# Prefetched mask tiles, a second set of accumulator banks, and two subtractions on GpSimd in a sandwich layer on eight cores

## The chip, the cores and the metric

The kernel runs on the eight cores of one Trainium2 chip, each with its own 2048 of the 16384 token rows and with all the weights. The metric is the device time of the slowest core in microseconds. Two runs of the kernel before took 3683.49 and 3685.18 us, median 3684.34 us.

## What is computed

```python
def reference(x, w1, mask, w2, bias):
    # mask is cut into blocks of 32x32; a block counts when its sum is > 0
    w_masked = w1 * elem_mask
    x = x + layernorm(einsum('bsk,nk->bsn', layernorm(x), w_masked))
    x = x + layernorm(einsum('bsi,oi->bso', layernorm(x), sign(w2)) + bias)
    return x
```

x is 2 x 8192 x 4096 in float32, w1, w2 and the int32 mask are 4096 x 4096. The products run in bf16.

## The kernel before

Each core takes its tokens in four chunks of 512 (`c`), a chunk in four token tiles of 128 (`tt`), and does the two layers of a chunk one after the other. A layer's weight comes in 16 slabs (`sl`) of 2 MB: `nsl = sl // 2` names one of eight groups of 512 output columns, `kh = sl % 2` a half of the contraction. A slab gives 64 matmuls (four token tiles by 16). The four token tiles of one `nsl` fill the four banks of `pmm`. After the second half DVE copies them to `ARAW` (L458 in layer 0, L461 with the bias in layer 1) and takes statistics (L469). The next `nsl` writes the same four banks, so its first matmul waits for that copy (`ev_at[(nsl - 1, tt)]`). The other four banks, `ptA` and `ptB`, are used for transposes and for small products of the mask.

**Chunk 0** makes the weights as it goes. SP loads float32 pieces of 512 KB into two buffers `WST` (L338). In layer 0, DVE multiplies a piece by the block mask `BTE` into the slab buffer `WSL` (L367), in layer 1 ACT takes the sign (L381). GpSimd stores each finished slab in DRAM as bf16 (L392), and chunks 1 to 3 load it from there (L407), into two slab buffers by turns.

**The mask chain** (`emit_mask_chain`) makes `BTE` for one `nsl`, eight times. For each of four row tiles of the mask GpSimd loads 2 MB (L228, into `OS` seen as int32), adds neighbours in five halving steps from 4096 to 128 columns (L238), ACT converts the 128 columns (L254), and PE and DVE reduce the rows (L267 to L284). The single staging tile and the working tile `MHI` are free for the next row tile once ACT has read `MHI` (`vAs`). At the end the 16 columns pass through DRAM (L297, L306). The chains of `nsl` 0 and 1 stand first in every queue, before the first normalization of x. The chain of `nsl` n+2 is placed behind slab 2n. So on DVE the multiplications of the slabs after it stand behind its four row tiles, and on GpSimd the chain stands behind the store of the slab before.

**Between layers.** `emit_p0` loads a chunk's x by halves of a token tile into two buffers `XS` and normalizes it. Once layer 0 is done, `emit_a2` does for each token tile and half: `ARAW *= r1` (L608), `XP = XS - m` (L610), `XP += ARAW` (L613), all on DVE. Then ACT squares and sums `XP` (L620), DVE works out the scale in some eleven operations of one column (L630 to L645), ACT normalizes into `HS` (L651), PE transposes into `ptA` and `ptB` (L204) and ACT copies to `HT` (L214). `emit_finalize` ends a chunk: for each token tile DVE waits until the output buffer `OS` has been stored (`sO`), then does `ARAW *= r3` (L695), `OS = XP - m` (L697), `OS += ARAW` (L700), and ACT issues the store (L706). The finalization of chunk c stands behind slab 0 of the next chunk on DVE, ahead of the copies out of `pmm`. That of the last chunk ends the program.

Of the kernel before, what the change touches and what calls it, by code (L numbers as in the profile page):

```python
# [19 lines left out]
D = 4096  # L20
# [11 lines left out]
SEMS = ["sW0", "sW1", "sWs0", "sWs1", "sX0", "sX1", "sM", "sC0", "sC1",  # L32
# [5 lines left out]
def build():  # L38
# [16 lines left out]
    with es:  # L55
# [161 lines left out]
        def emit_mask_chain(nsl, first):  # L217
# [3 lines left out]
            def _(g):  # L221
                for r in range(4):
                    rt = nsl * 4 + r
                    if rt == 0:
                        wt(g, bias_os_free)
                    else:
                        g.wait_ge(sem["vAs"], rt)
                    g.dma_start(OSi32[:, :], mask_d[rt * 128:(rt + 1) * 128, :]  # L228
                                ).then_inc(sem["sM"], 16)
                    cnt["sM"] += 16  # L230
                    g.wait_ge(sem["sM"], cnt["sM"])
                    spans = [(0, 2048), (2048, 1024), (0, 512), (2048, 256),
                             (0, 128)]
                    cur = OSi32[:, :]
# [179 lines left out]

        def emit_slab_mm(c, layer, sl, ready, su, ev_at, ht_mark, site,
                         pre_tt=None):
# [4 lines left out]
            def _(t):  # L421
# [4 lines left out]
                for tt in range(NT):  # L426
                    if kh == 0:
                        wt(t, ht_mark(tt))
                        if nsl > 0:
                            wt(t, ev_at.get((nsl - 1, tt)))  # L430
                        elif prev_ev[0] is not None:
                            wt(t, prev_ev[0][tt])
                    for j in range(KTS):
# [3 lines left out]
                        ins = t.matmul(pmm[:, tt * 512:(tt + 1) * 512],  # L437
# [11 lines left out]
            if kh == 1:  # L449
                @blk.vector  # L450
                def _(v):
                    wt(v, ("vFi", state["og"]))
                    ins = None
                    for tt in range(NT):
                        wt(v, mm_marks[tt])
                        dst = ARAW[:, tt * D + nsl * 512: tt * D + (nsl + 1) * 512]
                        if layer == 0:
                            ins = v.tensor_copy(dst,  # L458
                                                pmm[:, tt * 512:(tt + 1) * 512])
                        else:  # L460
                            ins = v.tensor_tensor(dst,  # L461
                                                  pmm[:, tt * 512:(tt + 1) * 512],
# [91 lines left out]
        def emit_a2(c, t0, ev_at):  # L554
            a2_load = {}

            @blk.gpsimd
            def _(g):
                for tt in range(NT):
                    for hf in range(2):  # L560
                        u = state["xs_uses"]
                        state["xs_uses"] += 1
                        g.wait_ge(sem["vXf"], u - 1)
                        sn = "sX%d" % (u % 2)
                        g.dma_start(XS[u % 2][:, :],  # L565
                                    x_d[t0 + tt * 128: t0 + (tt + 1) * 128,
                                        hf * 2048:(hf + 1) * 2048]
                                    ).then_inc(sem[sn], 16)
                        cnt[sn] += 16
# [238 lines left out]
```

## Time and profile before

| | |
|---|---|
| median of two runs | 3684.34 us |
| the profiled execution's own time | 3681.35 us |
| its span on the slowest core (core 3) | 3679.8 us |
| spans of the other cores | 3653.9 to 3668.1 us |
| mean granted TensorE clock, all cores | 0.793 to 0.799 |
| busy in the span | PE 54%, PEld 25%, DVE 24%, ACT 14%, POOL 9% |
| moved by DMA | 573 MB, 156 GB/s in the mean |

All stretches are in microseconds from the start of the span of core 3. PE is TensorE's matmuls and PEld its weight loads, DVE is VectorE, ACT ScalarE, POOL GpSimd, SP the queue of SyncE. A letter q behind an engine's name is its instruction queue. "Idle before" an instruction is followed by what ended the wait.

### The profile page before, as it was taken

What the parts mean: (1) busy time and instruction counts of PE and PEld (TensorE: products, weight loads), DVE (VectorE), ACT (ScalarE), POOL (GpSimd) and SP (SyncE); (2) the same over time, 40 slices, a digit from 0 to 9 for tenths busy, and PEclk for the clock granted to TensorE, in tenths of its full rate; (3) what the DMA queues carried; (4) which work ended last, traced back from release to release, by engine and by line L of the source; (5) the groups of instructions that cost most, each with busy time, mean ns of one, the idle gap of its engine ahead of it and who ended that gap; (6) DMA issues with size and microseconds to landing.
All of it is one profiled execution on the core that took longest, in us unless ns stands there. A gap on an engine that the chain in (4) does not pass through costs nothing.

```text
span 3679.8 us, 24392 instructions; the slowest of 8 cores (3653.9 to 3679.8 us)
## 1 busy us (share of the span) xinstructions
PE 1987.2 (54%) x9296; PEld 931.4 (25%) x9296; DVE 899.8 (24%) x1460; ACT 524.5 (14%) x364; POOL 344.1 (9%) x336
## 2 busy tenths in 40 slices
PE   1011321330334165654499299559919946983992
PEld 0010110110112122222244144224414422432441
DVE  0031220220224200112511411351141134223124
ACT  0030000000000633333100500110050020005000
POOL 2402132233220000000000000000000000000000
PEclk9996655665667587886699599779959977996996
DMA  2235644544555377776434334344333434341442
GB/s 94 101 122 176 184 129 169 172 147 141 184 159 208 92 239 229 242 227 211 182 143 149 125 115 160 137 183 153 144 114 137 160 137 183 144 153 69 160 151 101
DMA packets 72947, 573.16 MB, mean 156 GB/s; under 512 B 8800, under 2 KB 8816, under 8 KB 42112
## 3 DMA queue, kind: packets, MB, share of 16 engines
q1 hardware_dynamic: 50688, 335.57, 27.6%
q0 software_dynamic: 19840, 202.47, 15.2%
q10 hardware_dynamic: 2304, 33.56, 2.3%
q8 instruction: 76, 1.25, 0.1%
q14 instruction: 39, 0.32, 0.0%
HBM read 470.86 MB, written 100.70 MB: 155 GB/s over the span
## 4 chain that ended last, share of the span: by engine, by line
PE 36%; DMA 31%; DVE 11%; ACT 9%; POOL 7%; issue 4%; DVEq 0%; POOLq 0%; ACTq 0%; SPq 0%
PE pmm L437 35%; DMA WST<-w2s 10%; DMA OS<-mask 9%; DMA WST<-w1s 7%; POOL MHI L238 7%; DMA XS<-x 3%; DMA out<-OS 2%; DVE WSL L367 2%; DVE OS L700 2%; ACT WSL L381 2%; ACT HS L651 2%; ACT HS L620 2%; DVE BNST L508 1%; DVE OS L697 1%; PE ptA L204 1%
## 5 line engine op out<-in xcount | busy, mean ns | idle before, releaser
L437 PE MATMUL pmm<-WSL,HT 128*128 128x512 bf16 x8192 | 1846.7, 389 | 362.2 <-ACT WSL L381 195.5
L437 PEld LDWEIGHTS pmm<-WSL,HT 128*128 128x128 bf16 x8192 | 816.0, 100 | 1387.3 <-issue 472.0
L267 PE MATMUL ptB<-COLRED,P4T 128*4 128x128 bf16 x32 | 8.5, 265 | 680.3 <-ACT COLRED L254 680.3
L204 PE MATMUL ptA<-IDN,HS 128*128 128x128 bf16 x576 | 67.2, 310 | 551.0 <-ACT HS L651 304.5
L461 DVE TENSOR_TENSOR ARAW<-pmm,BIASF 128x512 bf16<-128x512 f32 x128 | 88.5, 691 | 991.8 <-PE pmm L437 991.8
L367 DVE TENSOR_TENSOR WSL<-WST,BTE 128x1024 bf16<-128x1024 f32 x128 | 155.7, 1223 | 210.6 <-DMA WST<-w1s 209.3
L458 DVE CAST ARAW<-pmm 128x512 bf16<-128x512 f32 x128 | 85.6, 688 | 487.6 <-PE pmm L437 487.0
L204 PEld LDWEIGHTS ptA<-IDN,HS 128*128 128x128 bf16 x576 | 58.6, 144 | 560.6 <-issue 560.6
L267 PEld LDWEIGHTS ptB<-COLRED,P4T 128*4 128x4 bf16 x32 | 2.6, 80 | 686.1 <-issue 686.1
L381 ACT ACTIVATE WSL<-WST 128x1024 bf16<-128x1024 f32 x128 | 135.1, 1056 | 249.4 <-DMA WST<-w2s 249.2
L280 DVE TENSOR_SCALAR BRT<-ptB 4x128 bf16<-4x128 f32 x32 | 8.9, 279 | 622.4 <-PE ptB L267 622.4
L469 DVE BATCH_NORM_STATS2 BNST<-ARAW 128x6 f32<-128x512 bf16 x256 | 158.3, 680 | 6.6
L620 ACT ACT_TABLE_LOAD x16 | 20.5, 1283 | 924.0 <-DVE XP L613 923.8
L238 POOL TENSOR_TENSOR MHI<-OS 128x2048 int32<-128x2048 int32 x32 | 114.8, 3588 | 309.7 <-DMA OS<-mask 309.7
L238 POOL TENSOR_TENSOR MHI<-MHI 128x1024 int32<-128x1024 int32 (+3 forms) x128 | 125.9, 984 | 18.7 <-POOL MHI L238 0.5
L565 POOL DMA_DIRECT2D XS<-x x32 | 19.5, 609 | 1006.8 <-DVE XP L613 930.4
L508 DVE BATCH_NORM_STATS2 BNST<-XS 128x6 f32<-128x512 f32 x128 | 78.8, 680 | 135.5 <-DMA XS<-x 135.5
L489 POOL DMA_DIRECT2D XS<-x x32 | 16.9, 530 | 735.2 <-ACT HS L540 681.4
L254 ACT ACT_TABLE_LOAD x8 | 10.3, 1283 | 514.2 <-POOL MHI L238 514.2
L214 ACT ACTIVATE HT<-ptA 128x2048 bf16<-128x2048 bf16 x36 | 67.6, 1877 | 79.5 <-PE ptA L204 79.5
L540 ACT ACT_TABLE_LOAD x4 | 5.1, 1283 | 511.4 <-DVE AUX L522 511.4
L700 DVE TENSOR_TENSOR OS<-OS,ARAW 128x4096 f32<-128x4096 f32 x16 | 70.8, 4425 | 1.7
(54 smaller groups left out, 742.6 us busy)
## 6 DMA issues: line engine op xcount, KB each, us to landing
WSL<-c1m SPq DMA_DIRECT2D x48, 2048.0 KB, 8.9
WSL<-c2m SPq DMA_DIRECT2D x48, 2048.0 KB, 8.8
WST<-w1s SPq DMA_DIRECT2D x128, 512.0 KB, 4.8
OS<-mask POOLq DMA_DIRECT2D x32, 2048.0 KB, 8.9
XS<-x POOLq DMA_DIRECT2D x64, 1024.0 KB, 6.0
WST<-w2s SPq DMA_DIRECT2D x128, 512.0 KB, 4.9
c1m<-WSL POOLq DMA_DIRECT2D x16, 2048.0 KB, 10.1
c2m<-WSL POOLq DMA_DIRECT2D x16, 2048.0 KB, 10.6
```

The lines of the kernel that those rows point to most:

```text
L204: ins = t.transpose(pt[:, j * 128:(j + 1) * 128], HS[:, ktg * 128:(ktg + 1) * 128], IDN[:, :])
L238: ins = g.tensor_tensor(MHI[:, dst_off:dst_off + dst_n], a[:, :, 0], a[:, :, 1], op=OP.add)
L367: ins = v.tensor_tensor(dst, src, mk, op=OP.mult)
L381: ins = s.activation(buf[:, j0 * 512:(j0 + KTQ) * 512], WST[(wfirst + q) % 2][:, :], AF.Sign)
L437: ins = t.matmul(pmm[:, tt * 512:(tt + 1) * 512], st_ap, mv_ap, start=(kh == 0 and j == 0), stop=(kh == 1 and j == KTS - 1))
L458: ins = v.tensor_copy(dst, pmm[:, tt * 512:(tt + 1) * 512])
L461: ins = v.tensor_tensor(dst, pmm[:, tt * 512:(tt + 1) * 512], BIASF[:, nsl * 512:(nsl + 1) * 512], op=OP.add)
L469: ins = v.bn_stats(BNST[:, sslot * 48 + nsl * 6: sslot * 48 + (nsl + 1) * 6], ARAW[:, tt * D + nsl * 512: tt * D + (nsl + 1) * 512])
L508: ins = v.bn_stats(bn[:, (hf * 4 + q) * 6: (hf * 4 + q + 1) * 6], xb[:, q * 512:(q + 1) * 512])
L620: ins = s.activation(HS[:, :], XP[:, tt * D:(tt + 1) * D], AF.Square, accum_out=XSQ[:, tt:tt + 1])
L651: ins = s.activation(HS[:, :], XP[:, tt * D:(tt + 1) * D], AF.Identity, bias=AUX[:, 8 + tt:8 + tt + 1], scale=RS[:, 8 + tt:8 + tt + 1])
L700: ins = v.tensor_tensor(OS[:, :], OS[:, :], srcr, op=OP.add)
```

## The change

Three things change, and the arithmetic stays the same.

1. In the mask chain there are two staging tiles for the mask, `OS` and the first 8192 columns of `XP`, used by turns and each with a semaphore of its own. The load of row tile r+1 is issued before the work on row tile r, and the wait for ACT's reading of `MHI` now stands before the first halving step and not before the load.
2. Except in layer 0 of chunk 0, the odd `nsl` accumulate in `ptA` and `ptB`, the even ones in `pmm`. A matmul then waits for the copy of `nsl - 2`. The first use of `ptA` and `ptB` in a layer waits until all transposes have been copied out.
3. The two subtractions (`XP = XS - m` and `OS = XP - m`) go from DVE to GpSimd. In `emit_a2` the loads of `XS` for a token tile stand just ahead of its subtractions in GpSimd's queue, where before all eight stood together. In `emit_finalize` the wait for the stored `OS` moves to GpSimd with the subtraction, so DVE's scaling no longer waits for it.

```diff
@@ emit_mask_chain, on GpSimd @@
-                for r in range(4):
+                stg = [OSi32, XP[:, 0:8192].bitcast(I32)]
+                ld = {}
+
+                def issue(r):
                     rt = nsl * 4 + r
                     if rt == 0:
                         wt(g, bias_os_free)
-                    else:
+                    sn = "sM" if rt % 2 == 0 else "sM1"
+                    g.dma_start(stg[rt % 2][:, 0:4096],
+                                mask_d[rt * 128:(rt + 1) * 128, :]
+                                ).then_inc(sem[sn], 16)
+                    cnt[sn] += 16
+                    ld[r] = (sn, cnt[sn])
+
+                issue(0)
+                for r in range(4):
+                    rt = nsl * 4 + r
+                    if r + 1 < 4:
+                        issue(r + 1)
+                    wt(g, ld[r])
+                    if rt > 0:
                         g.wait_ge(sem["vAs"], rt)
-                    g.dma_start(OSi32[:, :], mask_d[rt * 128:(rt + 1) * 128, :]
-                                ).then_inc(sem["sM"], 16)
-                    cnt["sM"] += 16
-                    g.wait_ge(sem["sM"], cnt["sM"])
                     spans = [(0, 2048), (2048, 1024), (0, 512), (2048, 256),
                              (0, 128)]
-                    cur = OSi32[:, :]
+                    cur = stg[rt % 2][:, 0:4096]
@@ emit_slab_mm @@
+        def acc_bank(use8, nsl, tt):
+            if use8 and nsl % 2 == 1:
+                pt = ptA if tt < 2 else ptB
+                return pt[:, (tt % 2) * 512:(tt % 2 + 1) * 512]
+            return pmm[:, tt * 512:(tt + 1) * 512]
...
-                        if nsl > 0:
-                            wt(t, ev_at.get((nsl - 1, tt)))
-                        elif prev_ev[0] is not None:
+                        if use8 and nsl == 1 and tt == 0:
+                            t.wait_ge(sem["vTe"], tr_base + 2 * NT)
+                            wt(t, bank_guard)
+                        prev_use = nsl - (2 if use8 else 1)
+                        if prev_use >= 0:
+                            wt(t, ev_at.get((prev_use, tt)))
+                        elif nsl == 0 and prev_ev[0] is not None:
                             wt(t, prev_ev[0][tt])
...
-                        ins = t.matmul(pmm[:, tt * 512:(tt + 1) * 512],
+                        ins = t.matmul(acc_bank(use8, nsl, tt),
@@ emit_a2: the loads of XS move into the loop over tt @@
+                @blk.gpsimd
+                def _(g, tt=tt):
...
+                    wt(g, chain1)
+                    wt(g, ("vFi", state["og"]))
                     mrs1 = AUX[:, 4 + tt:4 + tt + 1]
                     for hf in range(2):
                         u = a2_first + tt * 2 + hf
                         xbuf = XS[u % 2]
-                        wt(v, a2_load[(tt, hf)])
+                        wt(g, a2_load[(tt, hf)])
+                        dst = XP[:, tt * D + hf * 2048: tt * D + (hf + 1) * 2048]
+                        ins = g.tensor_scalar(dst, xbuf[:, :], mrs1, None,
+                                              OP.subtract)
+                        sub_mark[(tt, hf)] = inc(ins, "vPs", 1)
...
+                        wt(v, scale_mark[(tt, hf)])
+                        wt(v, sub_mark[(tt, hf)])
...
-                        vds_edge(v, ins)
-                        ins = v.tensor_scalar(dst, xbuf[:, :], mrs1, None,
-                                              OP.subtract)
-                        vds_edge(v, ins)
                         ins = v.tensor_tensor(dst, dst, srcr, op=OP.add)
@@ emit_finalize @@
                     wt(v, chain3)
-                    if my_og > 0:
-                        v.wait_ge(sem["sO"], 16 * my_og)
...
                     ins = v.tensor_scalar(srcr, srcr, r3, None, OP.mult)
-                    vds_edge(v, ins)
-                    ins = v.tensor_scalar(OS[:, :], XP[:, tt * D:(tt + 1) * D],
+                    fscale[tt] = inc(ins, "vDs", 1)
+
+                @blk.gpsimd
+                def _(g, tt=tt, my_og=my_og):
+                    wt(g, chain3)
+                    if my_og > 0:
+                        g.wait_ge(sem["sO"], 16 * my_og)
+                    mrs3 = AUX[:, 12 + tt:12 + tt + 1]
+                    ins = g.tensor_scalar(OS[:, :], XP[:, tt * D:(tt + 1) * D],
                                           mrs3, None, OP.subtract)
-                    vds_edge(v, ins)
+                    fsub[tt] = inc(ins, "vPs", 1)
@@ main loop @@
+                    use8 = not (c == 0 and layer == 0)
```

GpSimd's queue in the mask chain of `nsl` 0, before (from the first load to the end of the second row tile):

```order
L228 DMA OS<-mask 128x4096 [waits vBi]
L238 TENSOR_TENSOR MHI<-OS 128x2048 [waits sM]
L238 TENSOR_TENSOR MHI<-MHI 128x1024 [waits vPs]
L238 TENSOR_TENSOR MHI<-MHI 128x512 [waits vPs]
L238 TENSOR_TENSOR MHI<-MHI 128x256 [waits vPs]
L238 TENSOR_TENSOR MHI<-MHI 128x128 [waits vPs]
L228 DMA OS<-mask 128x4096 [waits vPs,vAs]
L238 TENSOR_TENSOR MHI<-OS 128x2048 [waits sM]
```

The same stretch with the change (up to the first step of the third row tile):

```order
L230 DMA OS<-mask 128x4096 [waits vBi]
L230 DMA XP<-mask 128x4096
L250 TENSOR_TENSOR MHI<-OS 128x2048 [waits sM]
L250 TENSOR_TENSOR MHI<-MHI 128x1024 [waits vPs]
L250 TENSOR_TENSOR MHI<-MHI 128x512 [waits vPs]
L250 TENSOR_TENSOR MHI<-MHI 128x256 [waits vPs]
L250 TENSOR_TENSOR MHI<-MHI 128x128 [waits vPs]
L230 DMA OS<-mask 128x4096 [waits vPs]
L250 TENSOR_TENSOR MHI<-XP 128x2048 [waits sM1,vAs]
```

The load of the second row tile has moved ahead of the first halving step, and each later load ahead of the wait for ACT (`vAs`).

TensorE's queue in layer 0 of chunk 1, `nsl` 0 and 1 (slabs 0 to 3), before:

```order
L437 MATMUL pmm<-WSL,HT 128x512 [waits sWs1]
L437 MATMUL pmm<-WSL,HT 128x512 x63
L420 UNCONDITIONAL_BRANCH
L437 MATMUL pmm<-WSL,HT 128x512 [waits sWs0,vTe,vEv]
L437 MATMUL pmm<-WSL,HT 128x512 x15
L437 MATMUL pmm<-WSL,HT 128x512 [waits vTe,vEv]
L437 MATMUL pmm<-WSL,HT 128x512 x15
```

and with the change:

```order
L459 MATMUL pmm<-WSL,HT 128x512 [waits sWs1]
L459 MATMUL pmm<-WSL,HT 128x512 x63
L438 UNCONDITIONAL_BRANCH
L459 MATMUL ptA<-WSL,HT 128x512 [waits sWs0,vTe,vEv]
L459 MATMUL ptA<-WSL,HT 128x512 x15
L459 MATMUL ptA<-WSL,HT 128x512 [waits vTe]
L459 MATMUL ptA<-WSL,HT 128x512 x15
L459 MATMUL ptB<-WSL,HT 128x512 [waits vTe]
L459 MATMUL ptB<-WSL,HT 128x512 x15
L459 MATMUL ptB<-WSL,HT 128x512 [waits vTe]
L459 MATMUL ptB<-WSL,HT 128x512 x15
```

The order is the same. The four token tiles of `nsl` 1 go to `ptA` and `ptB`, and what its first matmul waits for on `vEv` is no longer the copy of `nsl` 0.

DVE in the finalization of a token tile, two tiles in a row, before:

```order
L695 TENSOR_SCALAR ARAW<-ARAW,RS 128x4096 [waits vSt]
L697 TENSOR_SCALAR OS<-XP,AUX 128x4096 [waits vDs]
L700 TENSOR_TENSOR OS<-OS,ARAW 128x4096 [waits vDs]
L687 UNCONDITIONAL_BRANCH
L695 TENSOR_SCALAR ARAW<-ARAW,RS 128x4096 [waits vSt,sO]
L697 TENSOR_SCALAR OS<-XP,AUX 128x4096 [waits vDs]
L700 TENSOR_TENSOR OS<-OS,ARAW 128x4096 [waits vDs]
```

with the change, DVE and then GpSimd:

```order
L730 TENSOR_SCALAR ARAW<-ARAW,RS 128x4096 [waits vSt]
L743 UNCONDITIONAL_BRANCH
L748 TENSOR_TENSOR OS<-OS,ARAW 128x4096 [waits vDs,vPs]
L725 UNCONDITIONAL_BRANCH
L730 TENSOR_SCALAR ARAW<-ARAW,RS 128x4096 [waits vSt]
L743 UNCONDITIONAL_BRANCH
L748 TENSOR_TENSOR OS<-OS,ARAW 128x4096 [waits vDs,vPs]
```

```order
L739 TENSOR_SCALAR OS<-XP,AUX 128x4096 [waits vSt]
L733 UNCONDITIONAL_BRANCH
L739 TENSOR_SCALAR OS<-XP,AUX 128x4096 [waits vSt,sO]
L733 UNCONDITIONAL_BRANCH
L739 TENSOR_SCALAR OS<-XP,AUX 128x4096 [waits vSt,sO]
```

The subtraction and the wait for the stored `OS` (`sO`) have left DVE's queue. DVE's addition waits for GpSimd (`vPs`).

## Rows read from the trace of the kernel before

**Rows 1.** Busy time by stretch: its length, busy of each engine, TensorE clock, DMA share, GB/s

```profile
307.00:439.00 132.00, 34.67 (x136) 14.32 (x136) 25.93 (x32) 2.52 (x5) 37.42 (x32) 0.60 0.51 160
1284.00:1709.00 425.00, 253.01 (x1024) 105.83 (x1024) 38.74 (x59) 146.01 (x135) 9.56 (x18) 0.80 0.73 237
1709.00:1782.00 73.00, 13.89 (x127) 13.21 (x128) 35.83 (x95) 29.74 (x16) 4.95 (x8) 0.51 0.39 131
1782.00:1836.00 54.00, 28.31 (x132) 12.71 (x130) 29.84 (x12) 2.44 (x2) 0.00 (x0) 0.78 0.54 212
...
2122.00:2344.00 222.00, 222.00 (x1027) 100.38 (x1024) 38.73 (x59) 2.25 (x2) 0.00 (x0) 1.00 0.38 142
```

**Rows 2.** Chain of waits in the mask chain of nsl 2: start, duration, what

```profile
307.61 15.95 DMA OS<-mask
...
323.70 3.60 POOL MHI L238
...
331.40 0.41 POOL MHI L238
...
333.23 0.32 ACT COLRED L254
...
334.11 8.36 DMA OS<-mask
...
342.61 3.60 POOL MHI L238
...
386.22 0.41 POOL MHI L238
```

**Rows 3.** Groups by line and shape: busy us, mean ns, idle before and what ended it

```profile
L238 POOL TENSOR_TENSOR MHI<-OS 128x2048 int32<-128x2048 int32 x32 | 114.8, 3588 | 309.7 <-DMA OS<-mask 309.7
...
L238 POOL TENSOR_TENSOR MHI<-MHI 128x1024 int32<-128x1024 int32 x32 | 60.5, 1890 | 4.6
...
L697 DVE TENSOR_SCALAR OS<-XP,AUX 128x4096 f32<-128x4096 bf16 x16 | 37.6, 2353 | 1.7
```

**Rows 4.** Busy time while the first mask load of that chain runs, columns as in rows 1

```profile
308.00:323.00 15.00, 0.00 (x0) 0.00 (x0) 0.00 (x0) 0.00 (x0) 0.15 (x1) 0.50 0.95 310
```

**Rows 5.** Timeline where chunk 1 starts: start, duration, instruction, wait before it

```profile
1778.97 1.29 DVE L695 TENSOR_SCALAR ARAW<-ARAW,RS 128x4096 bf16<-128x4096 bf16 x1
1779.12 1.25 POOL L565 DMA_DIRECT2D XS<-x  x1 [1.46 <-ACT HS L544]
...
1782.19 28.12 PE L437 MATMUL pmm<-WSL,HT 128*128 128x512 bf16 x128
...
1794.25 1.29 DVE L695 TENSOR_SCALAR ARAW<-ARAW,RS 128x4096 bf16<-128x4096 bf16 x1 [7.00 <-DMA out<-OS]
...
1835.50 2.48 DVE L458 CAST ARAW<-pmm 128x512 bf16<-128x512 f32 x4 [0.17 <-DVE OS L700]
...
1836.34 4.00 PE L437 MATMUL pmm<-WSL,HT 128*128 128x512 bf16 x9 [26.02 <-DVE ARAW L458]
```

**Rows 6.** Who waited for whom: us in total, times, longest

```profile
PE pmm L437 <- DVE ARAW L458: 134.3, 10, 26.0
```

**Rows 7.** Timeline between the layers of chunk 1, token tiles 0 and 1

```profile
2047.54 0.53 POOL L565 DMA_DIRECT2D XS<-x  x1 [2.91 <-DVE XP L613]
...
2051.94 0.19 ACT L620 ACTIVATION_READ_ACCUMULATOR HS<-XP 128x1 f32 x1
...
2056.63 3.80 ACT L651 ACTIVATE HS<-XP,AUX,RS 128x4096 bf16<-128x4096 bf16 x1
...
2060.97 1.22 DVE L613 TENSOR_TENSOR XP<-XP,ARAW 128x2048 bf16<-128x2048 bf16 x1
...
2066.32 1.28 ACT L620 ACT_TABLE_LOAD   x1
```

**Rows 8.** DMA issues: size each, median us from issue to landing

```profile
XS<-x POOLq DMA_DIRECT2D x64, 1024.0 KB, 6.0
```

**Rows 9.** Chain of waits in the last finalization

```profile
3627.04 6.66 DMA out<-OS
```

More of the change, by code:

```diff
@@ L457, in _ @@
                         if layer == 0:
[L458 to L462 removed]
+                            ins = v.tensor_copy(dst, acc_bank(use8, nsl, tt))
+                        else:
+                            ins = v.tensor_tensor(dst, acc_bank(use8, nsl, tt),
                                                   BIASF[:, nsl * 512:(nsl + 1) * 512],
@@ L555, in emit_a2 @@
             a2_load = {}
[L557 to L569, printed above, removed]
-                        a2_load[(tt, hf)] = (sn, cnt[sn])
-            a2_first = state["xs_uses"] - 8
+            a2_first = state["xs_uses"]
             @blk.vector
@@ L595, in emit_a2 @@
             for tt in range(NT):
+                scale_mark = {}
                 @blk.vector
@@ L599, in _ @@
                     r1 = RS[:, 4 + tt:4 + tt + 1]
+                    for hf in range(2):
+                        srcr = ARAW[:, tt * D + hf * 2048:
+                                    tt * D + (hf + 1) * 2048]
+                        ins = v.tensor_scalar(srcr, srcr, r1, None, OP.mult)
+                        scale_mark[(tt, hf)] = inc(ins, "vDs", 1)
+                sub_mark = {}
+                @blk.gpsimd
+                def _(g, tt=tt):
+                    for hf in range(2):
+                        u = state["xs_uses"]
+                        state["xs_uses"] += 1
+                        g.wait_ge(sem["vXf"], u - 1)
+                        sn = "sX%d" % (u % 2)
+                        g.dma_start(XS[u % 2][:, :],
+                                    x_d[t0 + tt * 128: t0 + (tt + 1) * 128,
+                                        hf * 2048:(hf + 1) * 2048]
+                                    ).then_inc(sem[sn], 16)
+                        cnt[sn] += 16
+                        a2_load[(tt, hf)] = (sn, cnt[sn])
+                    wt(g, chain1)
+                    wt(g, ("vFi", state["og"]))
                     mrs1 = AUX[:, 4 + tt:4 + tt + 1]
@@ L603, in _ @@
                         xbuf = XS[u % 2]
-                        wt(v, a2_load[(tt, hf)])
+                        wt(g, a2_load[(tt, hf)])
[3 more added lines that the diff above has]
+                        sub_mark[(tt, hf)] = inc(ins, "vPs", 1)
+                @blk.vector
+                def _(v, tt=tt):
+                    for hf in range(2):
+                        wt(v, scale_mark[(tt, hf)])
+                        wt(v, sub_mark[(tt, hf)])
                         dst = XP[:, tt * D + hf * 2048: tt * D + (hf + 1) * 2048]
@@ L757, in build @@
                 prev_ev[0] = {tt: ev_at[(7, tt)] for tt in range(NT)}
+                if layer == 0:
+                    l0_ev_last = ev_at[(7, NT - 1)]
                 if layer == 0:
```

23 lines of the change are left out of this document (17 added, 6 removed).

## The prediction

> **What bounds the kernel now.** I read the busy time by stretch first, then the chain of waits inside the stretches in which TensorE is idle. In layers 1 of chunks 1 to 3 TensorE is never idle: 1024 matmuls in 222 us at full clock [rows 1]. Nothing in the change touches that. The time to be won lies elsewhere.
>
> Layer 0 of chunk 0 runs in periods of about 132 us, in which TensorE is busy for 35 us, GpSimd for 37 us and the DMA engines for half the time [rows 1]. Nobody is full, so the work is in series. The chain of waits shows how: a mask load, GpSimd's five halving steps, ACT's conversion, and only then the next load [rows 2]. GpSimd waits 309.7 us for 32 loads [rows 3]. DVE's multiplications of the next two slabs stand behind the whole chain in DVE's queue and take the rest of the period.
>
> Layer 1 of chunk 0 is 425 us at 237 GB/s with two small buffers in flight [rows 1]. Extra accumulator banks don't help it.
>
> At the start of chunks 1 to 3 TensorE does `nsl` 0 in 28.12 us and then stands for 26.02 us, because DVE reaches the copies out of `pmm` only behind the finalization [rows 5]. All ten such waits of the kernel are 134.3 us, the longest 26.0 [rows 6]; three of them are these.
>
> **Part 1, the mask chain.** In `nsl` 2 the first step starts at S = 323.70 and the last ends at 386.22 + 0.41 = 386.63, that is S + 62.9 [rows 2]. The work on one tile is 331.81 - 323.70 = 8.1 us. Afterwards, tile by tile:
> - Tile 0 ends at S + 8.1. Its conversion with the table load is done at 333.55, S + 9.9 [rows 2]. Tile 1 has long been queued: the first load landed after 15.95 us behind the slab's store, and together these 4 MB ran at 310 GB/s [rows 2, 4], at which the next 2.1 MB need 6.8 us. So tile 1 starts at S + 10.0 and ends at S + 18.1.
> - Tile 2 was issued at S + 8.2 and lands after 0.5 (issue) and 8.4 us [rows 2] at S + 17.1. It starts after the conversion of tile 1 (0.6 us) at S + 18.7 and ends at S + 26.8.
> - Tile 3 is issued at S + 18.1 and lands at S + 27.0. It starts at S + 27.4 and ends at S + 35.5.
>
> The gain is 62.9 - 35.5 = 27.4 us for a chain. Load and work are now about equally long, so what is late next is either, by tenths. I take 27 for loads that meet those of other cores. All eight chains are on the path: two stand ahead of the first normalization, six ahead of DVE's multiplications. That makes -216 us. Bounds: if loads cost nothing, a tile costs 8.7 us and the gain is 28 each (-224). If a prefetched load takes as long as load and work together take now, the gain is 0.
>
> **Part 2, the banks.** TensorE can now go on with `nsl` 1 for another 128 matmuls (27.8 us at 222 us for 1024) and needs the copy of `nsl` 0 at 1782.2 + 28.1 + 27.8 = 1838.1. DVE has the first tile out at 1836.2 [rows 5]. So the wait goes, with 1.9 us to spare, if the finalization gets no longer. The layer now takes 54 + 196 = 250 us, of which 196 for 896 matmuls, against 222 us undisturbed [rows 1]: 26 us of wait and 2 of matmuls at the lower granted clock after it (0.78 in the stretch with the wait). The gain is 28 us each, -84 us for three. The seven other waits for a copy, 56 us in all, belong to `nsl` 1 to 7 of layer 0 in chunk 0, where the banks stay as they are. The added wait for the transposes' copies ends before `nsl` 0 is done.
>
> **Part 3, the subtractions.** The trace shows no `TENSOR_SCALAR` on GpSimd. The nearest row is its addition of two inputs: 3588 ns for 2048 columns and 1890 for 1024 [rows 3], so 1.66 ns for a column and 0.2 us for each instruction. One input less to read could halve the slope: f = 3.6 us for 4096 columns and s = 1.9 for 2048. That is my value. Above stands the full two-input price, f = 7.0 and s = 3.6. Below stands DVE's own 2.35 us for 4096 columns [rows 3].
>
> The Trainium skill, "GPSIMD Engine Reference", section "Engine selection", calls one-input operations on GpSimd roughly line-rate, against about half of VectorE's speed with two inputs. The trace has only the second kind, and by its slope it agrees with my halving; by line rate the sum would be the same within a few microseconds.
>
> Finalization. A round is now a store (6.66 us [rows 9]), DVE's scaling 1.29, subtraction 2.35 and addition 4.43, in all 15.1 with the gaps. With the change DVE scales during the store, and the round is 6.66 + f + 4.43 + 0.4 = 15.1 with f = 3.6. So nothing is won on this path: the scaling that is hidden pays for the slower subtraction. The first round has scaling and subtraction in parallel or, if they get in each other's way, in series, +1.1 us. At the start of chunks 1 to 3 this uses the 1.9 us to spare, and I allow 1 us in all for it. At the end: +1. With f = 7.0 each round is 3.4 longer. That is +14 at the end, and in each of three chunks a wait of 14 - 2 = 12 us stays with its slow matmuls, so the banks gain 14 instead of 28.
>
> Between the layers. ACT is the busy one after the first tile: it copies, squares, waits for DVE's scale, normalizes, and DVE has `XP` of the second tile ready at 2062.2, 4.1 us ahead of ACT's next square at 2066.3 [rows 7]. GpSimd can be late by that. For the first tile two subtractions and one addition, 2 x 1.9 + 1.2 plus gaps, stand against 6.9 us now, and I cost it at nothing. But the loads of `XS` for tile 1 are issued by 2047.54 and land after about 6.0 us [rows 7, 8], at 2053.5. GpSimd now subtracts at once, while DVE works out the scale of tile 0 (2052.1 to 2055.3). Whether the two disturb each other is seen at 1779.12: GpSimd's DMA issue took 1.25 us instead of 0.53 while DVE scaled `ARAW` [rows 5, 7]. I add 1.5 us, four times, +6. With s = 3.6 it is 3 for the first tile and up to 6 for the scale, +36.
>
> The Trainium skill, "SBUF — State Buffer", section "Who interferes with whom", has a rule against this part: a VectorE instruction with two SBUF inputs and a GpSimd instruction that reads SBUF block each other for the whole instruction. The row at 1779.12 agrees with a lock held to the end of the other's instruction. If it held for every tile it would be the fourth rival below.
>
> **Sum.** -216 - 84 + 1 + 1 + 6 = -292. Against the profiled execution's 3681.35 (span 3679.8) that is 3389; the median of the runs stands 3 us above it, so 3392.
>
> **The rivals.**
> - *GpSimd pays the two-input price* (f 7.0, s 3.6): -216 - 42 + 14 + 36 = -208, 3476 us. For it: the only rows of GpSimd. Against it: half of the reading falls away. 0.22.
> - *The prefetch is hidden by bandwidth.* All cores stream the mask at once, a load takes as long as load and work did, and only parts 2 and 3 count: -76, 3608 us. For it: between loads the engines now rest, so no stretch of this chain shows 2 MB every 9 us. Against it: 310 GB/s held for 15 us [rows 4], and 237 for 425 us [rows 1], where the chain would need 233. 0.07. Halfway (13 us a load) is 3500.
> - *Slower than before.* GpSimd's subtraction becomes the bound of every finalization and of every tile between layers. Each microsecond of f above 3.6 costs 12 in three chunks, 4 at the end and 16 between the layers (16 tiles of two halves, once the slack is used), so 32. It decides from f = 12.7 us, where 292 are eaten up, 1.8 times the two-input price. At f = 15 it gives 3757 us. Only a conversion between bf16 and float32 in GpSimd's software could do that. 0.02.
> - *GpSimd and DVE in turns at every tile*: each scale between layers waits for both subtractions, 3.8 us for 16 tiles, +61 in place of +6: 3447 us. Against it: from the second tile on, the loads land some 10 us before DVE works out a scale. 0.07.
>
> **How the numbers follow.** My forecast has 0.62. Its own range is 3372 to 3420. The range takes in the two-input price and reaches to 3485. Below, all bounds in the change's favour (-224, -84, DVE's price) give 3370, so 3365. Faster by over 2%, about what a measurement of this kernel tells from no change, means under 3611: all cases but the slower one and a part of the second, 0.95; within 2% 0.03; slower 0.02.
>
> **What would show it.** In the changed profile GpSimd's wait for mask loads should fall from 310 us to about 120, the periods of chunk 0 from 132 to 105, and layer 1 should start near 1068 instead of 1284. The 26 us wait of TensorE in chunks 1 to 3 should be gone or under 3 us. The new lines 636 and 739 on GpSimd give s and f directly: f over 5 says the first rival. The rounds of the last finalization should be 15 us. Mask loads of over 11 us would make part 1 wrong.

## The result, and the profile after

The changed kernel takes 3595.66 us (median of 11 runs, 3576.81 to 3630.58), the kernel before 3688.5 us beside it (10 runs, 3680.58 to 3724.49). The ratio is 0.9725, with an interval from 0.9696 to 0.9755, so about 100 us are won (93 between the two medians). Ratios here compare only the runs in which no half of the chip's cores ran late at a lower granted clock, and medians take all. I had predicted 3392 us, a gain of 292, and a range that ends at 3485. The sign is right, and two thirds of the gain are missing. The profiled execution took 3576.8 us (span 3575.3 on core 0), and the stretches below are its own.

Where the time went, stage by stage (core 3 before, core 0 after). The last two columns sum to -102 found and -292 predicted; between the two profiled executions lie 104.5 us.

| stage | before | after | difference | predicted |
|---|---|---|---|---|
| start to the last matmul of layer 0 in chunk 0 | 1170 | 956 | -214 | -216 |
| layer 0 to layer 1, in each of four chunks | 114, 90, 90, 90 | 133, 108, 108, 107 | +73 | +6 |
| layer 1 of chunk 0 | 425 | 424 | -1 | 0 |
| layer 0 of chunks 1 to 3, each | 250 | 254 | +13 in all | -83 in all |
| layer 1 of chunks 1 to 3, each | 222 | 222 | 0 | 0 |
| last matmul to the end | 69 | 96 | +27 | +1 |

The same busy times by stretch as in [rows 1]: a period of the mask chain, layer 1 of chunk 0, then of chunk 1 layer 0, the time between the layers and layer 1, and the end. Columns: length, busy us of PE, PEld, DVE, ACT, POOL, TensorE clock, DMA share, GB/s.

```profile
362.00:467.00 105.00, 33.14 (x133) 14.04 (x136) 25.63 (x32) 2.52 (x5) 36.55 (x30) 0.66 0.62 201
1089.00:1512.00 423.00, 255.43 (x1001) 106.82 (x1020) 38.75 (x59) 146.01 (x135) 9.05 (x18) 0.78 0.73 237
1585.00:1839.00 254.00, 222.53 (x1003) 100.41 (x1021) 66.83 (x68) 1.32 (x1) 39.25 (x6) 0.94 0.45 166
1839.00:1947.00 108.00, 14.24 (x128) 13.55 (x130) 45.01 (x85) 52.81 (x27) 49.72 (x16) 0.55 0.27 97
1947.00:2169.00 222.00, 220.38 (x1004) 100.13 (x1022) 38.99 (x60) 2.07 (x2) 0.00 (x0) 1.00 0.39 142
3479.00:3576.00 97.00, 0.00 (x0) 0.00 (x0) 28.79 (x29) 0.00 (x0) 43.48 (x4) 0.53 0.21 87
```

The period fell from 132 to 105 us, and DMA is busy for 0.62 of it where it was 0.51. Between the layers POOL is busy for 49.7 us where it had 4.2 us of DMA issues. At the end it has 43.5 of 97 us.

The chain of waits of the same mask chain (`nsl` 2) shows the new order:

```profile
362.32 14.54 DMA OS<-mask
377.06 3.60 POOL MHI L250
...
386.58 0.32 ACT COLRED L266
387.05 3.60 POOL MHI L250
396.26 3.62 POOL MHI L250
...
412.69 0.41 POOL MHI L250
```

The first step starts at S = 377.06. Tile 1 starts 0.15 us after ACT has read tile 0, with no load between them, where [rows 2] had 8.36 us of load. The last step ends at 413.1, S + 36.0, against S + 62.9 before.

Four groups of the changed kernel, with [rows 3] to compare. Columns: busy us, mean ns | idle before, and what ended it.

```profile
L636 POOL TENSOR_SCALAR XP<-XS,AUX 128x2048 bf16<-128x2048 f32 x32 | 181.2, 5664 | 610.7 <-DVE AUX L182 564.1 <-DMA XS<-x 46.6
L739 POOL TENSOR_SCALAR OS<-XP,AUX 128x4096 f32<-128x4096 bf16 x16 | 172.9, 10804 | 465.8 <-DVE AUX L182 308.8 <-DMA out<-OS 156.9
L748 DVE TENSOR_TENSOR OS<-OS,ARAW 128x4096 f32<-128x4096 f32 x16 | 70.8, 4425 | 247.6 <-POOL OS L739 247.4 <-DVE ARAW L730 0.2
L665 DVE TENSOR_TENSOR NEWT<-MV 128x1 f32<-128x1 f32 x16 | 31.1, 1942 | 167.2 <-ACT HS L655 167.2
```

The finalization's subtraction takes 10.8 us, where DVE had 2.35 and I had put 3.6. The one between the layers takes 5.66 where I had put 1.9. DVE's addition waits 247.4 us for them in total. The last line is an operation of DVE on one column that takes 1942 ns, which the experiments explain.

Who waited for whom (total us, times, longest), as in [rows 6]:

```profile
DVE OS L748 <- POOL OS L739: 247.4, 15, 22.2
PE pmm L459 <- DVE ARAW L480: 145.9, 10, 30.6
POOL MHI L250 <- DMA OS<-mask: 108.5, 8, 16.2
ACT L686 <- DVE AUX L680: 93.1, 16, 9.2
```

GpSimd's waits for the mask fell from 32 (309.7 us) to 8 (108.5). TensorE's waits for the copies did not fall at all (145.9 us, 134.3 before [rows 6]). The timeline of the start of chunk 1 shows why:

```profile
1580.73 10.61 POOL L739 TENSOR_SCALAR OS<-XP,AUX 128x4096 f32<-128x4096 bf16 x1 [15.98 <-DVE AUX L182]
1580.85 11.57 DVE L730 TENSOR_SCALAR ARAW<-ARAW,RS 128x4096 bf16<-128x4096 bf16 x1 [0.30 <-DVE AUX L182]
1592.60 4.42 DVE L748 TENSOR_TENSOR OS<-OS,ARAW 128x4096 f32<-128x4096 f32 x1 [0.17 <-DVE ARAW L730]
...
1604.27 10.61 POOL L739 TENSOR_SCALAR OS<-XP,AUX 128x4096 f32<-128x4096 bf16 x1 [12.93 <-DMA out<-OS]
1614.99 4.43 DVE L748 TENSOR_TENSOR OS<-OS,ARAW 128x4096 f32<-128x4096 f32 x1 [16.77 <-POOL OS L739]
...
1654.74 10.61 POOL L739 TENSOR_SCALAR OS<-XP,AUX 128x4096 f32<-128x4096 bf16 x1 [17.18 <-DMA out<-OS]
...
1670.05 2.48 DVE L480 CAST ARAW<-pmm 128x512 bf16<-128x512 f32 x4 [0.17 <-DVE OS L748]
```

```profile
1670.88 29.84 PE L459 MATMUL pmm<-WSL,HT 128*128 128x512 bf16 x126 [30.27 <-DVE ARAW L480]
```

The finalization takes 89.3 us (1580.73 to 1670.05) where it took 56.5 (1778.97 to 1835.50 [rows 5]). TensorE does `nsl` 0 and 1 without a wait, as planned, in 56 us, and then stands 30.27 us at `nsl` 2. The banks moved the wait by one `nsl`, and the longer finalization brought a wait of its own of about the same length. The four subtractions take 4 x 8.3 = 33 us more than DVE's did. That the scaling now runs during a store gives 4 us back, and slower stores take as much again: here they land after 7.0 to 12.4 us, and on the whole kernel their median rose from 7.1 to 8.4.

### The profile page after: what moved, and what is told of

It is laid out like the page before. It is cut to its first block, busy times and chain, and to the rows that moved or that the text cites. A ratio compares the mean times of both kernels' runs of the same rounds, so it can differ in the third digit from the quotient of the medians.

```text
span 3575.3 us, 24253 instructions; the slowest of 8 cores (3559.9 to 3575.3 us)
## 1 busy us (share of the span) xinstructions
PE 1983.5 (55%) x9127; PEld 934.0 (26%) x9296; DVE 891.2 (25%) x1412; ACT 524.4 (15%) x364; POOL 696.6 (19%) x384
## 4 chain that ended last, share of the span: by engine, by line
PE 35%; DMA 26%; POOL 13%; DVE 11%; ACT 9%; issue 5%; POOLq 0%; DVEq 0%; ACTq 0%; SPq 0%
PE pmm L459 17%; DMA WST<-w2s 10%; PE ptA L459 8%; PE ptB L459 8%; DMA WST<-w1s 8%; POOL MHI L250 7%; POOL OS L739 4%; DMA OS<-mask 3%; DMA out<-OS 3%; DMA XS<-x 3%; DVE WSL L379 2%; DVE OS L748 2%; ACT WSL L393 2%; ACT HS L686 2%; ACT HS L655 2%
## 5 line engine op out<-in xcount | busy, mean ns | idle before, releaser
L459 PE MATMUL pmm<-WSL,HT 128*128 128x512 bf16 x4523 | 1055.9, 395 | 282.4 <-DVE ARAW L480 145.9
L459 PEld LDWEIGHTS pmm<-WSL,HT 128*128 128x128 bf16 x4608 | 464.0, 101 | 867.7 <-issue 367.2
L459 PE MATMUL ptA<-WSL,HT 128*128 128x512 bf16 x1750 | 410.9, 391 | 92.1 <-ACT WSL L393 89.2
L459 PE MATMUL ptB<-WSL,HT 128*128 128x512 bf16 x1750 | 393.7, 379 | 2.2
L636 POOL TENSOR_SCALAR XP<-XS,AUX 128x2048 bf16<-128x2048 f32 x32 | 181.2, 5664 | 610.7 <-DVE AUX L182 564.1
L739 POOL TENSOR_SCALAR OS<-XP,AUX 128x4096 f32<-128x4096 bf16 x16 | 172.9, 10804 | 465.8 <-DVE AUX L182 308.8
L459 PEld LDWEIGHTS ptA<-WSL,HT 128*128 128x128 bf16 x1792 | 178.9, 100 | 316.4 <-issue 117.5
L459 PEld LDWEIGHTS ptB<-WSL,HT 128*128 128x128 bf16 x1792 | 175.3, 98 | 211.5
L482 DVE TENSOR_TENSOR ARAW<-pmm,BIASF 128x512 bf16<-128x512 f32 x64 | 44.3, 692 | 528.3 <-PE pmm L459 528.3
L748 DVE TENSOR_TENSOR OS<-OS,ARAW 128x4096 f32<-128x4096 f32 x16 | 70.8, 4425 | 247.6 <-POOL OS L739 247.4
L482 DVE TENSOR_TENSOR ARAW<-ptA,BIASF 128x512 bf16<-128x512 f32 x32 | 22.1, 692 | 376.9 <-PE ptA L459 376.9
## 6 DMA issues: line engine op xcount, KB each, us to landing
OS<-mask POOLq DMA_DIRECT2D x16, 2048.0 KB, 10.6
XP<-mask POOLq DMA_DIRECT2D x16, 2048.0 KB, 12.8
```

The costliest lines, as they stand in the source:

```text
L459: ins = t.matmul(acc_bank(use8, nsl, tt), st_ap, mv_ap, start=(kh == 0 and j == 0), stop=(kh == 1 and j == KTS - 1))
L636: ins = g.tensor_scalar(dst, xbuf[:, :], mrs1, None, OP.subtract)
L739: ins = g.tensor_scalar(OS[:, :], XP[:, tt * D:(tt + 1) * D], mrs3, None, OP.subtract)
L748: ins = v.tensor_tensor(OS[:, :], OS[:, :], srcr, op=OP.add)
```

## The experiments

A layer's length is counted from its first to its last matmul, and times "of before" are those of the kernel before on the same chip.

**1. Parts 1 and 2 without part 3.** Both subtractions and their waits go back to DVE, the loads of `XS` stand together again.

```diff
-                        ins = g.tensor_scalar(dst, xbuf[:, :], mrs1, None,
+                        ins = v.tensor_scalar(dst, xbuf[:, :], mrs1, None,
...
-                    ins = g.tensor_scalar(OS[:, :], XP[:, tt * D:(tt + 1) * D],
+                    ins = v.tensor_scalar(OS[:, :], XP[:, tt * D:(tt + 1) * D],
```

> Parts 1 and 2 only, both subtractions back on VectorE. Price theory (GpSimd's subtraction, 2.6 ns for a column, gave back the rest): the 26 us waits of TensorE are gone, 3384 us, 0.918 of before. Rival (stores of the output now collide with slab loads, because TensorE no longer stops, and this keeps a wait of its own at the start of chunks 1 to 3): the fourth copy still comes 15 to 20 us late, 3430 to 3440 us, 0.93.

Measured: 3410.96 us, ratio 0.9274 (0.9227 to 0.932); the three runs behind the ratio took 3390, 3398 and 3424 us, the fourth 3474. By its ratio this is above the 0.918 of the price theory and at the 0.93 of the rival. The layers tell the two apart: layer 0 of chunks 1 to 3 is 221 to 222 us on nearly all cores, so no copy comes late there, and the banks do all that part 2 promised once the finalization is short. What is over the expected time lies, in part, in stretches at a lower clock: two cores, 0 and 1, had two layers each of 232 to 249 us. Core 1, one such layer, its first 166 and its last 83 us:

```profile
2482.00:2648.00 166.00, 166.00 (x640) 69.03 (x638) 23.03 (x35) 2.44 (x2) 0.00 (x0) 0.82 0.32 114
2648.00:2731.00 83.00, 83.00 (x386) 37.59 (x384) 15.72 (x24) 0.00 (x0) 0.00 (x0) 1.00 0.43 152
```

TensorE waits for nothing in either. In the first stretch the granted clock is 0.82 and a matmul takes 259 ns (166.00 / 640), in the second the clock is 1.00 and a matmul takes 215 ns. I come back to it in the last section.

**2 to 4. Each part alone.** Part 1 alone, part 2 alone, part 3 alone, each against before.

```diff
@@ 2: part 1, without the banks @@
-                        ins = t.matmul(acc_bank(use8, nsl, tt),
+                        ins = t.matmul(pmm[:, tt * 512:(tt + 1) * 512],
@@ 3: part 2, with one staging tile for the mask @@
-                    cur = stg[rt % 2][:, 0:4096]
+                    cur = OSi32[:, :]
@@ 4: part 3 on the kernel before @@
-                    ins = v.tensor_scalar(OS[:, :], XP[:, tt * D:(tt + 1) * D],
+                    ins = g.tensor_scalar(OS[:, :], XP[:, tt * D:(tt + 1) * D],
```

> Part 1 only. Price theory: -214 us as in the changed profile, 3472 us, 0.942; TensorE's 26 us waits stay. Rival: the same, so this run only gives the size of part 1 alone.

> Part 2 only. Price theory: 28 us for each of chunks 1 to 3, -84 us, 3602 us, 0.977. Rival (store and slab load collide): -30 to -40 us, 0.990, with rounds of the finalization of 18 us and more in chunks 1 to 3.

> Part 3 only, on one set of banks. Price theory: +18 us between the layers four times (72), +27 at the end, and about +30 at the start of each of chunks 1 to 3, where the longer finalization stands in full ahead of the copies (90): +190 us, 3878 us, 1.051. Rival (GpSimd's operations are only slow because mask loads or other banks changed something else): under +100 us.

Measured: part 1 alone 3470.67 us, ratio 0.9454 (0.9427 to 0.948). Part 2 alone 3605.55, 0.9824 (0.9775 to 0.9874). Part 3 alone 3853.03, 1.0498 (1.047 to 1.0526). All three stand within 0.6% of the time before from where they were expected. For part 2 alone the interval leaves out both the expected 0.977 and the rival's 0.990, and it reaches over the 2% line; here too the layers decide. With part 2 alone the layers 0 of chunks 1 to 3 are 221 to 223 us (but for one layer of two cores at a lower clock); with part 3 alone they are 275 to 279. So the subtractions cost 5% by themselves, and the change is two gains with a loss in it. The three parts add up: -5.5, -1.8 and +5.0% make -2.2%, against the -2.75% of the whole.

The same holds inside a layer 0 of chunks 1 to 3. It takes 250 us before, 222 with the banks alone, 277 with the subtractions alone and 254 with both. The banks win 28 us without part 3 and 23 us with it; part 3 costs 27 and 32 us.

**5. Is it the price of the instruction or the mutual blocking?** GpSimd starts a tile's subtraction only after DVE has worked out the scale of the tile before. This is the changed kernel with one wait more:

```diff
+                    if tt > 0:
+                        wt(g, chain2[tt - 1])
```

> The changed kernel, but GpSimd's subtractions for token tile t wait until VectorE has worked out the scale of tile t-1. Lock theory (a GpSimd operation and a VectorE operation with two inputs from SBUF hold each other up to the end of the other): L665 takes 0.16 us instead of 1.9 in the mean, the wait of ACT for the scale falls from 9.2 us at most to 3.4, but the subtractions start later and end about 2 us after ACT could square the next tile; in all -3 to -15 us against the changed kernel (0.996 to 0.999). Rival (VectorE's small operations are slow for another reason, or only the price counts): L665 still 1.9 us, and the kernel 20 us or more slower than the changed one.

Measured: 3573.61 us, ratio 0.9746 (0.9719 to 0.9773), which isn't told apart from the changed kernel's 0.9725 (0.9696 to 0.9755). The expected gain of 3 to 15 us is not seen, and neither is the rival's loss. The groups show that the blocking is real and that it only moved. First the changed kernel between the layers of chunk 1, then this one:

```profile
1865.95 10.85 POOL L636 TENSOR_SCALAR XP<-XS,AUX 128x2048 bf16<-128x2048 f32 x2 [3.48 <-DMA XS<-x]
...
1866.62 3.04 DVE L665 TENSOR_TENSOR NEWT<-MV 128x1 f32<-128x1 f32 x1 [5.24 <-ACT HS L655]
...
1870.02 0.16 DVE L671 TENSOR_TENSOR NEWT<-NEWT 128x1 f32<-128x1 f32 x1
...
1871.86 3.22 DVE L168 TENSOR_TENSOR RS<-RS,NEWT 128x1 f32<-128x1 f32 x1
...
1875.68 1.28 ACT L686 ACT_TABLE_LOAD   x1 [9.17 <-DVE AUX L680]
```

```profile
L667 DVE TENSOR_TENSOR NEWT<-MV 128x1 f32<-128x1 f32 x16 | 2.5, 159 | 84.1 <-ACT HS L657 84.1
L638 POOL TENSOR_SCALAR XP<-XS,AUX 128x2048 bf16<-128x2048 f32 x32 | 202.4, 6328 | 653.6 <-DVE AUX L182 563.4 <-DVE AUX L682 90.2
```

```profile
1864.48 6.60 DVE L610 TENSOR_SCALAR ARAW<-ARAW,RS 128x2048 bf16<-128x2048 bf16 x2
1864.83 12.60 POOL L638 TENSOR_SCALAR XP<-XS,AUX 128x2048 bf16<-128x2048 f32 x2 [7.48 <-DVE AUX L682]
```

The two-input operation on one column falls from 1942 to 159 ns. In exchange the subtraction rises from 5664 to 6328 ns and DVE's scaling of `ARAW` (L610) from 1525 to 3342, since these two now meet. ACT's waits for a scale fall from 93.1 to 52.3 us, about the value before (52.8); instead it now waits for `XP` at twelve tiles, 3.3 us each, 40 us in all. A duration in the trace holds the time for which an instruction was blocked by the other engine.

The Trainium skill, "SBUF — State Buffer", section "Who interferes with whom", says that a DVE instruction with two inputs in SBUF and a GpSimd instruction that reads SBUF contend for shared ports, whose lock is exclusive and held for a whole instruction. L665 and L168 have two inputs and are held up, which agrees. But they are not held up for the whole subtraction, and here the measurement decides. The first one starts at 1865.95 and the second at 1871.37, and each takes 5.4 us. L665 ends at 1869.66 and L168 at 1875.08, both 3.71 us after such a start, and L671, also with two inputs, takes its usual 0.16 us inside the rest of the first. On this core all sixteen operations held up in this way end 3.71 us after the start of a subtraction. DVE's scaling reads one tile only, so these rows of two-input operations say nothing of it. It is held up nearly to the end: L730 at 1580.85 ends 1.1 us after the subtraction beside it, and its own work is 1.28.

**6. The price by itself.** The kernel before, with ten operations of GpSimd appended at its very end, one at a time, while every other engine rests. They write scratch only, and the kernel's own time (3735 us, one run) says nothing here. The ten operations and the wait for the last store make its end 59 us longer, where 30 to 50 were expected.

```diff
+            for n in (1024, 2048):
+                one(g.tensor_scalar(xb[:, 0:n], xf[:, 0:n], m, None, OP.subtract))
...
+            one(g.tensor_tensor(OS[:, 0:2048], xf[:, :], xg[:, :], op=OP.add))
...
+            one(g.tensor_copy(xb[:, 0:2048], xf[:, :]))
```

> The kernel before, with ten GpSimd operations alone at its very end, each waiting for the one before; scratch results only. Lock theory of the price (GpSimd's subtraction is slow because VectorE works beside it): alone, 2048 columns float32 to bf16 take about 2 to 3.6 us. Price theory: 5.4 us alone too, 2.6 ns a column. If a scalar from memory is what costs, the form with an immediate scalar is far under 5.4; if the conversion costs, float32 to float32 is; if all GpSimd float arithmetic costs this much, the addition of two float32 inputs is at 5 us or over against 3.6 for int32. The kernel itself is longer by the sum of the ten, 30 to 50 us.

```profile
3674.15 2.85 POOL L777 TENSOR_SCALAR XP<-XS,AUX 128x1024 bf16<-128x1024 f32 x1 [328.06 <-DMA out<-OS]
3677.16 5.44 POOL L777 TENSOR_SCALAR XP<-XS,AUX 128x2048 bf16<-128x2048 f32 x1 [0.17 <-POOL XP L777]
...
3688.36 10.62 POOL L779 TENSOR_SCALAR OS<-XP,AUX 128x4096 f32<-128x4096 bf16 x1 [0.17 <-POOL OS L779]
3699.15 5.43 POOL L780 TENSOR_SCALAR OS<-XS,AUX 128x2048 f32<-128x2048 f32 x1 [0.17 <-POOL OS L779]
3704.75 5.43 POOL L781 TENSOR_SCALAR XP<-XP,AUX 128x2048 bf16<-128x2048 bf16 x1 [0.17 <-POOL OS L780]
3710.34 5.36 POOL L782 TENSOR_SCALAR OS<-XS 128x2048 f32<-128x2048 f32 x1 [0.15 <-POOL XP L781]
3715.84 4.49 POOL L783 TENSOR_TENSOR OS<-XS 128x2048 f32<-128x2048 f32 x1
3720.48 4.04 POOL L784 TENSOR_TENSOR XP<-XP 128x2048 bf16<-128x2048 bf16 x1
3724.67 1.89 POOL L785 CAST XP<-XS 128x2048 bf16<-128x2048 f32 x1
```

A subtraction costs 2.53 ns for a column ((5.44 - 2.85) / 1024, and (10.62 - 5.44) / 2048), and it's the same for float32, for bf16, for a conversion between them, and for a constant in place of the column `m`. So neither the conversion nor DVE's work beside it is the cause. Why the subtraction takes this long is not shown. It is dearer than an addition of two whole inputs (4.49 and 4.04 us). Only the cast, which also reads one input, runs at 1.89 us.

The Trainium skill, "GPSIMD Engine Reference", section "Engine selection", has one-input operations roughly at line rate. The cast is not far from that: it takes 1.89 us where DVE's subtraction of the same shape took 1.31 us before. `TENSOR_SCALAR` with 5.44 us doesn't agree, and the measurement decides.

**7. Neither engine pays for a subtraction.** Parts 1 and 2, and the subtraction becomes the second operation of DVE's scaling. It leaves `ARAW * r - m`, rounded to bf16 with m in it, where before m was taken from x. In the finalization the wait for the stored `OS` also moves behind the scaling (against experiment 1):

```diff
-                    if my_og > 0:
-                        v.wait_ge(sem["sO"], 16 * my_og)
...
-                    ins = v.tensor_scalar(srcr, srcr, r3, None, OP.mult)
-                    vds_edge(v, ins)
-                    ins = v.tensor_scalar(OS[:, :], XP[:, tt * D:(tt + 1) * D],
-                                          mrs3, None, OP.subtract)
+                    ins = v.tensor_scalar(srcr, srcr, r3, mrs3,
+                                          OP.mult, OP.subtract)
...
+                    if my_og > 0:
+                        v.wait_ge(sem["sO"], 16 * my_og)
-                    ins = v.tensor_tensor(OS[:, :], OS[:, :], srcr, op=OP.add)
+                    ins = v.tensor_tensor(OS[:, :], XP[:, tt * D:(tt + 1) * D],
+                                          srcr, op=OP.add)
```

> Parts 1 and 2, and no subtraction at all: VectorE's scaling takes m in the same instruction (ARAW*r - m) and the sum is then x + ARAW. The value of m is rounded with ARAW to bf16, otherwise the result is the same. Price theory: the finalization's round is store 6.7 + addition 4.4 = 11.3 us instead of 15.1, so -15 us at the end against parts 1 and 2 alone, and -1 to -2 us between layers four times: 3362 us, 0.911 of before. Rival (the addition from bf16 and float32 costs what the subtraction cost): no better than parts 1 and 2 alone, 3384 us.

Measured: 3370.15 us, ratio 0.9182 (0.9169 to 0.9196), 8 us over the expected 3362. The layers of chunks 1 to 3 are 221 to 224 us on all cores. The last finalization:

```profile
3331.96 4.42 DVE L716 TENSOR_TENSOR OS<-XP,ARAW 128x4096 f32<-128x4096 bf16 x1 [5.27 <-DMA out<-OS]
3336.30 1.34 DVE L711 TENSOR_SCALAR ARAW<-ARAW,RS,AUX 128x4096 bf16<-128x4096 bf16 x1
3342.86 4.42 DVE L716 TENSOR_TENSOR OS<-XP,ARAW 128x4096 f32<-128x4096 bf16 x1 [5.22 <-DMA out<-OS]
```

Two operations in one instruction take 1.34 us, against 1.29 for the scaling alone [rows 5]. A round is the store and one addition, 10.9 us instead of 15.1. Of these 4.2 us the subtraction is 2.4; most of the rest is the scaling, which now runs during the store. So the gain at the end is not the fusion's alone, and no run tells the two apart.

**8 and 9. Which of the two subtractions costs what.** The changed kernel with only the finalization's subtraction back on DVE, and with only the one between the layers back.

```diff
@@ 8: emit_finalize @@
-                    ins = g.tensor_scalar(OS[:, :], XP[:, tt * D:(tt + 1) * D],
+                    ins = v.tensor_scalar(OS[:, :], XP[:, tt * D:(tt + 1) * D],
@@ 9: emit_a2 @@
-                        ins = g.tensor_scalar(dst, xbuf[:, :], mrs1, None,
+                        ins = v.tensor_scalar(dst, xbuf[:, :], mrs1, None,
```

> The changed kernel with the finalization's subtraction back on VectorE; the subtraction between the layers stays on GpSimd. If the two places of part 3 add up: parts 1 and 2 plus four times 18 us, 0.925 + 0.020 = 0.945 of before, about 3465 us, and TensorE has no wait for a copy in chunks 1 to 3. Rival (the longer time between layers hides behind something once the finalization is short): no more than 0.93.

> The changed kernel with the subtraction between the layers back on VectorE; the finalization's stays on GpSimd. If they add up: parts 1 and 2 plus 27 us at the end and 32 us for each of chunks 1 to 3, 0.925 + 0.033 = 0.958, about 3510 us, and the layers 0 of chunks 1 to 3 take 254 us as in the changed kernel. Rival: under 0.945.

Measured: 3455.56 us, ratio 0.9429 (0.9399 to 0.946), with layers 0 of 221 to 228 us and 17 to 20 us more between the layers. And 3510.81 us, 0.9565 (0.9539 to 0.9592), with layers 0 of 252 to 257 us. Both stand where the sum of the two places put them (0.945 and 0.958). Of 3688 us, the finalization's move costs (0.9725 - 0.9429) x 3688 = 109 us and the other's (0.9725 - 0.9565) x 3688 = 59 us. Each carries about 15 us from the two intervals, and the stage table has 3 x 32 + 27 = 123 and 73. Together they are 168 us; taking both away (experiments 1 and 10) gives 166 and 184.

**10 and 11. The first and the seventh again, side by side.** No edit.

> Parts 1 and 2 only, as in the first experiment, whose median was 27 us over the expected 3384 while two cores of its profile had layers at a granted clock of 0.81. If those stretches belong to runs and not to the kernel, this one can come out at 3370 to 3385 us; if they belong to a TensorE that no longer stops in chunks 1 to 3, they are there again in one core or another, and the median is over 3395 us.

> The version without a subtraction once more, beside parts 1 and 2 on the same chip: 15 to 20 us under them, 0.915 to 0.92 of before, if stretches at a lower clock come to both alike; more than 30 us under them if they come only to the other.

Measured: 3390.8 us, ratio 0.9227 (0.9201 to 0.9252), and 3372.56 us, 0.918 (0.9154 to 0.9207). The tenth fell between the two times that its expectation told apart, so the fork stays undecided; its profile has no stretch at a lower clock in chunks 1 to 3. In microseconds it is 7 over the expected 3384, and in its profile the slowest core's layer 1 of chunk 0 is 435 us, where the profile before had 425. The eleventh is 18 us under the tenth, the 15 to 20 that were expected if such stretches come to both alike. The version without any separate subtraction is the best here: 8.2% under before, and 5.6% under the changed kernel (0.918 / 0.9725).

## Why the prediction was right and wrong

**Part 1, right.** The working gave S + 35.5 for the end of a chain and the trace has S + 36.0; the period is 105 us as foretold, and the layer ends 214 us earlier for 216. Layer 1 of chunk 0 starts at 1088.6 and not near 1068, since the time between the layers ahead of it grew by 18 us. One sign was set wrongly: "Mask loads of over 11 us would make part 1 wrong". The loads into `XP` have a median of 12.8 us from issue to landing, those into `OS` 10.6. They are issued early enough to take that long: only the first load of each chain is waited for (8 waits of 32).

**Part 2, right.** The working said that the wait goes with 1.9 us to spare "if the finalization gets no longer". Experiments 1, 3 and 8 show the 28 us of each layer. In the changed kernel the finalization is 33 us longer, and a wait of 30 us stands at the next `nsl`. The condition failed and not the banks: without them the wait is 54.9 us (experiment 4) and the layer 277 us in place of 254.

**Part 3, the step that failed.** It is the sentence "One input less to read could halve the slope: f = 3.6 us for 4096 columns and s = 1.9". They measured 10.6 and 5.4. Nothing stood behind the halving: the trace before had no one-input operation of GpSimd, so its slope couldn't agree with it, though the prediction says that it does. The upper bound failed too: I took the two-input price as the worst case, and it isn't one (experiment 6). The rival "GpSimd pays the two-input price" (3476 us) had the direction and still lies 120 us below. What I'd called slower than before had f = 15 and its turning point at 12.7; the measured 10.6 is much nearer to that than to my value.

With the right f, the working of the finalization holds, and that of the time between the layers doesn't:
- A round of the last finalization, 6.66 + f + 4.43 + 0.4 with f = 10.6 and the store of 6.28 us, is 21.7; the chain of waits has 21.66:

```profile
3498.86 4.44 DVE OS L748
3503.37 6.28 DMA out<-OS
3509.80 10.62 POOL OS L739
3520.52 4.44 DVE OS L748
```

- At the chunk starts the rise of 7.0 us, four times, is 28 us, as much as the banks win. Measured are 32 us beside what was expected (254 against 222); the slower stores are most of the difference.
- Between the layers I had 16 us for each microsecond of f, which gives 112. It was 67 beyond my 6, and for other reasons. At the first tile of a chunk ACT starts its square 14.4 us after DVE's first scaling, where it was 7.0, because two long subtractions stand in series there: 29 us in four chunks. At the later tiles no subtraction is late at all; ACT goes from its copies to its square without a wait. Late is the scale. ACT's waits for it rose from 52.8 to 93.1 us, 40 in all, and the held-up operations of DVE account for them: 28.5 us at L665 and 12.3 at L168. I had put 1.5 us a chunk, 6 in all, for this.

So 32 us for each microsecond, over 7.0 us, would have given 3392 + 224 = 3616, some 20 us above the measured median and 39 above the profiled execution. The time between the layers is more than all of that: 118 us by this rule, 73 measured.

**The rivals.** Hidden by bandwidth: fallen, as a chain of 36.0 us shows. GpSimd and DVE in turns at every tile: half right, and it has more than half of what was lost between the layers. The blocking exists where a subtraction starts beside a two-input operation (3.04 us for one column), and ACT waits up to 9.2 us for a scale. What I held against it was that the loads land some 10 us before DVE works out a scale. That was misread. In the kernel before, tile 2's second load and the end of tile 1's scale are

```profile
2062.75 0.53 POOL L565 DMA_DIRECT2D XS<-x  x1 [2.91 <-DVE XP L613]
...
2074.66 0.15 DVE L645 TENSOR_SCALAR AUX<-AUX 128x1 f32<-128x1 f32 x1
```

so with 6.0 us it lands at 2068.8, 6 us before that end and 2.6 before the scale's first operation (2071.4), and two subtractions of 5.4 us run over the whole of it. Only the first of the two loads is there nearly 10 us before the end. The row at 1779.12, which the prediction holds beside the rule, is a DMA issue beside a scaling with one input; it showed that the engines hold each other up, and not that a two-input operation does. Taking the meeting away (experiment 5) wins nothing that can be measured, because the long instruction then meets another one and ends later itself.

## What to carry to other kernels

Before work is moved to an engine, measure that very operation there, alone: another operation's row isn't a bound for it, even if it reads more. When a stretch comes out as long as before (here 254 us after 250), test the parts alone: it can hold a gain of 23 and a loss of 32 us. And before a cheap operation is moved, ask whether it can ride as the second operation of an instruction that is there already: that gave 3370 us here, against 3391 to 3411 with the subtraction on DVE and 3596 with it on GpSimd.

## What the runs showed of the hardware that was not expected

- GpSimd's `TENSOR_SCALAR` costs 2.53 ns for a column for all types tried, more than its addition of two inputs, while its cast of 2048 columns takes 1.89 us.
- Whoever started first went first. In the finalization at the start of chunk 1, GpSimd's first subtraction started 0.12 us ahead of DVE's scaling of 4096 columns, and the scaling took 11.57 us instead of 1.28. In the three other finalizations DVE started first, and GpSimd's first subtraction took 11.63 to 11.64 us instead of 10.61. The blocked time is counted as busy in either engine's rows.
- A two-input operation of DVE was held up until 3.71 us after the start of a subtraction of 5.42 us, and no longer. A scaling with one input was held up nearly to the subtraction's end.
- Two neighbouring cores at a time (0 and 1, 6 and 7, 4 and 5) ran uninterrupted matmuls at a granted clock of 0.80 to 0.82 in nearly the same stretch, for some 50 to 170 us, and such a layer was 11 to 28 us longer. It was seen in the profiles of experiments 1, 3 and 6, the last of which has the queues of the kernel before, so it isn't the banks' doing. Other profiles of the same and of other kernels have none. What brings it about stayed open and was not tried.
